# Scoring two time steps at once in four 32-column tiles, with the gated recurrence 14 slots behind

## The reference, cut to what matters

```python
hist, news = inputs[:, :-1, :], inputs[:, -1, :]
hs = _gru(hist, gru_W, gru_U, gru_b)                       # 50 sequential steps
emb = concat([hs, news - hs, news, hs * news])             # attention
a = relu(emb @ att_W1 + att_b1)                            # 512 -> 128
a = relu(a @ att_W2 + att_b2)                              # 128 -> 64
ats = sigmoid(a @ att_W3 + att_b3)                         # 64 -> 1, the score
def au_step(h, xs):                                        # gated recurrence, 50 steps
    u, r = sigmoid(xu_t + h @ au_Uu), sigmoid(xr_t + h @ au_Ur)
    c = tanh(xc_t + r * (h @ au_Uc))
    u_ = at_t * u
    return (1.0 - u_) * h + u_ * c
x = batchnorm(concat([h_final, news]))                     # then the head:
x = leaky(x @ d_W1 + d_b1); x = leaky(x @ d_W2 + d_b2); y = sigmoid(x @ f_W + f_b)
```

## Time and profile before

| | us |
|---|---|
| median of 3 runs | 1956.56 (1956.45 to 1956.91) |
| the profiled execution | 1956.07 |
| its span | 1954.2 |
| PE busy | 1930.7 (99%) |
| POOL, DVE, ACT busy | 1627.2, 1501.8, 1458.8 |

### The profile page before, as it was taken

The page is one execution under the profiler, slowest core; times in us unless marked ns, Lnnn a source line. Parts: engine busy times, 40 slices in busy tenths (PEclk is TensorE's granted clock), DMA queues, the critical chain, the costliest instruction groups (busy, mean ns, idle before and its releaser), DMA issues. The chain is left out here.

```text
span 1954.2 us, 29732 instructions
## 1 busy us (share of the span) xinstructions
PE 1930.7 (99%) x9190; PEld 859.3 (44%) x9190; DVE 1501.8 (77%) x2355; ACT 1458.8 (75%) x2466; POOL 1627.2 (83%) x1387
## 2 busy tenths in 40 slices
PE   8999999999999999999999999999999999999988
PEld 3344444444444444444444444444444444444433
DVE  7877777777777777777777777777777777777875
ACT  7877777777777777777777777777777777777764
POOL 7788888888888888888888888888888888888762
PEclk9999999999999999999999999999999999999999
DMA  3121111111111111111111121111111111111010
GB/s 127 50 71 49 49 70 52 50 49 70 48 48 70 49 51 52 70 48 48 54 65 48 49 69 53 49 49 70 48 48 70 48 52 50 70 48 48 33 44 22
DMA packets 37577, 108.12 MB, mean 55 GB/s; under 512 B 4329, under 2 KB 4585, under 8 KB 31153
## 3 DMA queue, kind: packets, MB, share of 16 engines
q1 hardware_dynamic: 37410, 107.57, 15.5%
q10 hardware_dynamic: 144, 0.26, 0.0%
HBM read 107.39 MB, written 0.42 MB: 55 GB/s over the span
## 5 line engine op out<-in xcount | busy, mean ns | idle before, releaser
L949 PE MATMUL ps<-h_hi,w_hi 128*128 128x512 f16 x1384 | 525.2, 380 | 11.4 <-DVE g L722 6.7
L951 PE MATMUL ps<-h_hi,w_lo 128*128 128x512 f16 x1384 | 524.5, 379 | 0.0
L950 PE MATMUL ps<-h_lo,w_hi 128*128 128x512 f16 x1384 | 524.5, 379 | 0.0
L304 POOL TENSOR_TENSOR hn_lo<-hn,hn_hi 128x512 f16<-128x512 f32 x200 | 232.6, 1163 | 183.4 <-ACT hn_hi L420 183.3
L298 POOL TENSOR_TENSOR hn<-h,news 128x512 f32<-128x512 f32 x200 | 255.3, 1277 | 74.6 <-DVE h L846 74.5
L569 ACT ACTIVATE ps<-gt,p_rest 128x512 f32<-128x512 f32 x196 | 135.3, 690 | 216.4 <-DVE gt L843 216.4
L370 POOL TENSOR_TENSOR gus<-gu,score 128x512 f32<-128x512 f32 x197 | 249.9, 1268 | 5.2 <-DMA score<-score_rows 3.6
L363 POOL TENSOR_TENSOR g_lo<-g,g_hi 128x512 f16<-128x512 f32 x196 | 228.0, 1163 | 18.9 <-ACT g_hi L594 17.6
L834 DVE TENSOR_TENSOR gt<-gr,ps 128x512 f32<-128x512 f32 x196 | 134.7, 687 | 140.2 <-ACT gr L597 140.2
L317 POOL TENSOR_TENSOR x_lo<-x,x_hi 128x512 f16<-128x512 f32 x196 | 227.4, 1160 | 15.1 <-ACT x_hi L440 10.6
L377 POOL TENSOR_TENSOR d<-h,hc 128x512 f32<-128x512 f32 x186 | 236.9, 1274 | 0.4 <-ACT hc L590 0.4
(11 more groups left out here) (131 smaller groups left out, 3728.2 us busy)
## 6 DMA issues: line engine op xcount, KB each, us to landing
score<-score_rows SPq DMA_DIRECT2D x50, 1024.0 KB, 4.6
x<-in_xs SPq DMA_DIRECT2D x199, 256.0 KB, 3.1
news<-in_xs SPq DMA_DIRECT2D x4, 256.0 KB, 5.1
score_rows<-s_rows SPq DMA_DIRECT2D x50, 8.0 KB
p_rest<-in_pack_rest SPq DMA_DIRECT2D x1, 776.0 KB, 6.6
p_att<-in_pack_att SPq DMA_DIRECT2D x1, 290.0 KB, 5.2
x<-in_xs ACTq DMA_DIRECT2D x1, 256.0 KB, 4.1
p_gru<-in_pack_gru SPq DMA_DIRECT2D x1, 195.0 KB, 4.3
```

The lines of the kernel that those rows point to most:

```text
L304: g.tensor_tensor(hn_lo[:, k, :], hn[:, k, :], hn_hi[:, k, :], ALU.subtract).then_inc(hnlo_ready, 1)
L949: m.matmul(ps[:, bank, :], w_hi[:, w, :], hi, start=start, stop=False)
L950: m.matmul(ps[:, bank, :], w_hi[:, w, :], lo, start=False, stop=False)
L951: return m.matmul(ps[:, bank, :], w_lo[:, w, :], hi, start=False, stop=stop)
```

## The change

- `BLOCK` = 8 items (two steps) are scored together. Layer-two activations get four buffers instead of two (`a2_hi`, `a2_lo`), `w3_pair` is 128x32, and `scores` makes 8 matmuls once in eight slots, in four column tiles of 32. `s_rows` then holds eight rows; SP stores them once per two steps and spreads them by two DMAs of four rows each, with a semaphore each; `score` has eight chunks.
- LAG 10 -> 14, HIST (ring of h parts, and loop body) 12 -> 16 slots: the loop covers slots 20 to 195 in 11 passes; EARLY = 18. So slots 4 to 13 are without gated part, 14 to 17 with 6 matmuls of it, 18 to 199 are full, 200 to 214 hold the rest.
- Start: `p_gru` comes in two DMAs (reset weights and biases first). Item 0 is done with three fp32 matmuls straight from `p_gru` and `x32`, without splits. The update gate of the first four items has four PSUM banks. WARM 10 -> 7. The second load of x chunk 0 waits for `z_pe`.
- Slots from 200 are written apart (`late`): products `gxh` of the gated part alternate between two banks (`gxh_bank`), so PE waits for the state two items back and not one; the last scores are made at slot 203 in bank B_A1.
- Batch norm: three Newton rounds of three small DVE operations; two of the small operations in each of slots 18, 19 and 196 to 199, in the middle of the slot, three more in slots 200 to 202. The scale goes into the first head weights (`w_d1`, split in fp16), the shift into the bias by four tiny matmuls; `news_bn` and the scaled states are gone.
- Head: the first layer uses split fp16 products, except two fp32 ones for the last state. ACT computes the leaky branch from PSUM, DVE the other and the maximum. `head_out` runs once for all chunks, at four 32-row offsets of one bank.

```diff
-    LAG = 10
-    HIST = 3 * NC
-    LOOP_LO = 4 * NC
+    LAG = 14
+    HIST = 4 * NC
+    BLOCK = 2 * NC
+    LOOP_LO = 5 * NC
...
-            def scores(count):
+            def scores(count, bank=B_SCORE):
                 for p in range(2):
                     pe.wait_ge(a2lo_ready[p], count)
                 for part in (a2_hi, a2_lo):
-                    for p in range(2):
-                        done = m.matmul(ps[p * H:(p + 1) * H, B_SCORE, :], w3_pair[:, :], part[:, p, :],
+                    for q in range(NC):
+                        done = m.matmul(ps[32 * q:32 * (q + 1), bank, :], w3_pair[:, :], part[:, q, :],
                                         start=part is a2_hi, stop=part is a2_lo)
-                done.then_inc(score_pe, NC)
+                done.then_inc(score_pe, BLOCK)
...
+            def spread_scores(scored, stored, first_used, second_used):
                 sp.wait_ge(s_ready, scored)
+                if first_used is not None:
+                    sp.wait_ge(gus_ready, first_used)
+                sp.dma_start(score_rows[:, :], s_rows[0:P:P // BLOCK, :]).then_inc(rows_stored, 16)
                 sp.wait_ge(rows_stored, stored)
-                sp.dma_start(score[:, :, :], score_rows.partition_broadcast(P)).then_inc(score_landed, 16)
+                sp.dma_start(score[:, 0:NC, :], score_rows[0:NC, :].partition_broadcast(P)).then_inc(score_landed[0], 16)
+                if second_used is not None:
+                    sp.wait_ge(gus_ready, second_used)
+                sp.dma_start(score[:, NC:, :], score_rows[NC:, :].partition_broadcast(P)).then_inc(score_landed[1], 16)
...
+            pe.wait_ge(gru_landed, 16)
+            pe.wait_ge(x_landed[0], 16)
+            first_item(B_R0[0], "Wr", r_pe)
+            pe.wait_ge(input_landed, 16)
+            first_item(B_XH0[0], "Wh", xh_pe)
+            first_item(B_Z0[0], "Wz", z_pe)
...
+            def late(low):
+                item = low - LAG
...
+                if low == ITEMS:
+                    pe.wait_ge(g_ready, item)
+                elif low == ITEMS + 1:
+                    pe.wait_ge(t1_ready, ITEMS)
+                else:
+                    pe.wait_ge(g_ready, item - 1)
+                split_product(gxh_bank(item), GW_C, *hg, start=True, stop=True).then_inc(gxh_pe, 1)
...
+            def head_1_state(c):
+                pe.wait_ge(glo_ready, ITEMS - NC + c + 1)
+                for k in range(2):
+                    split_product(B_D1[c][k], D_1 + k, g_hi[:, c, :], g_lo[:, c, :], start=False, stop=True).then_inc(d1_pe, 1)
+            def head_out():
+                pe.wait_ge(y2_ready, NC)
+                for c in range(NC):
+                    done = m.matmul(ps[32 * c:32 * c + 1, B_F, :], p_rest[:, PACK_REST["F"]], y2[:, c, :],
+                                    start=True, stop=True)
```

More of the change, by code:

```diff
@@ L271, in _ @@
                 load_step(3, c)
-                if c == 2:
-                    spread_scores(NC, None, 16)
-            with sp.Fori(4, T) as step:
+            for c in range(NC):
+                load_step(4, c)
+                if c == 1:
+                    spread_scores(BLOCK, 16, None, None)
+            for c in range(NC):
+                load_step(5, c)
+            xs_next = xs[1:, :, :]
+            with sp.Fori(6, T, 2) as step:
                 for c in range(NC):
@@ L621, in head_2 @@
                 act.wait_ge(d2_pe, c + 1)
[L622 to L634 removed]
+                a.activation(y2p[:, c % 2, :], ps[:, B_D2[c % 2], :], ACT.Identity,
+                             bias=b_leak[:, 2:3], scale=LEAKY).then_inc(y2p_ready, 1)
@@ L636, in _ @@
+            for s in range(ITEMS, ITEMS + LAG):
+                late(s)
+            late(ITEMS + LAG)
+            head_1(1)
+            head_2(0)
+            head_1(2)
+            head_2(1)
+            head_1(3)
+            head_2(2)
+            head_2(3)
+            head_out()
         @block.vector
@@ L811, in slot @@
                 if pairs_of(low - 1):
-                    low_2(1, paired(s0 + (off - 1)))
+                    low_2(1, low - 1, paired(s0 + (off - 1)))
                 if has(low):
@@ L943, in _ @@
+            for s in range(ITEMS, ITEMS + LAG):
+                late(s)
+            late(ITEMS + LAG)
+            for k in range(2):
+                head_1(1, k)
+            head_2(0)
+            for k in range(2):
+                head_1(2, k)
+            head_2(1)
+            for k in range(2):
+                head_1(3, k)
+            head_2(2)
+            head_2(3)
         @block.tensor
@@ L1243, in _ @@
-            for s in range(LOOP_HI, LAST):
-                slot(s - s % NC, s % NC)
-            head_1_state(0)
-            for c in range(1, NC + 3):
-                if c < NC:
-                    head_1_news(c, 0)
-                    head_1_news(c, 1)
-                    head_1_state(c)
-                if 0 <= c - 1 < NC:
-                    head_2(c - 1)
-                if 0 <= c - 2 < NC:
-                    head_out(c - 2)
+                m.matmul(ps[:, bank, :], dw2[:, 0, :], y1[c % 2][:, 0, :], start=True, stop=False)
@@ new lines, in head_2, with head_out @@
+                m.matmul(ps[:, bank, :], dw2[:, 1, :], y1[c % 2][:, 1, :], start=False, stop=True).then_inc(d2_pe, 1)
+            def head_out():
+                pe.wait_ge(y2_ready, NC)
+                for c in range(NC):
+                    done = m.matmul(ps[32 * c:32 * c + 1, B_F, :], p_rest[:, PACK_REST["F"]], y2[:, c, :],
+                                    start=True, stop=True)
+                done.then_inc(f_pe, 1)
+            for s in range(LOOP_HI, ITEMS):
+                slot(s - s % NC, s % NC)
@@ L1257 @@
+            for s in range(ITEMS, ITEMS + LAG):
+                late(s)
+            head_1_news(1, 1)
+            head_1_state(1)
+            head_2(0)
+            head_1_news(2, 0)
+            head_1_news(2, 1)
+            head_1_state(2)
+            head_1_news(3, 0)
+            head_1_news(3, 1)
+            head_2(1)
+            last_state()
+            head_2(2)
+            head_2(3)
+            head_out()
 def kernel(**inputs):
```

578 lines of the change are left out of this document (366 added, 212 removed).

## The result

| | before | after |
|---|---|---|
| median, us | 1956.56 (1956.08 to 1958.45, 5 runs) | 1948.19 (1946.67 to 1948.36, 5 runs) |
| span of the profiled execution | 1954.2 | 1946.4 |

The ratio is 0.9954, with a 95% interval of 0.994 to 0.9969: 8.4 us faster, where 19.6 were forecast. The time lies in the range, the mechanism that put it there is not the forecast's.

What follows compares the result with a forecast made beforehand. PE was taken to bound the loop, dependencies the rest; -10.8 + 2.3 + 0 + 1.1 - 1.0 - 3.5 - 0.4 - 6.8 = -19.1 us from 1956.07 gave 1937, range 1928 to 1949.

Steps and rivals of the forecast that it cites:

- What bounds the kernel: Inside the loop PE is always busy, so only the number of matmuls and changes of form count; outside, dependencies.
- part 1: Scores: four 32-column tiles run side by side, -10.8 us; one more change of form per two steps, +2.3.
- part 3: LAG 14: four added early slots bring idle time, +1.1 us; the longer loop body makes no difference.
- The rival that says so: Loop body outgrows what an engine holds, instruction fetches stall each back edge: 1945 to 1963 us, chance 0.08.
- Part 4: Start: item 0 by three fp32 products of 0.86 each, four update-gate banks: -1.0 us, bounds 0 and -2.5.
- the bound that was named 0: End of the start's range in which ACT's chain begins as before and nothing is gained.
- Part 5: Batch norm operations spread over six slots: -3.5 us, leaving 1.0 in slots 196 to 199, 0.3 in 18 and 19.
- Part 6: Gated tail from state 199: DVE's order sets 4.24 us per gated state, sum 71.4, change -0.4 us.
- Part 7: Head, last gated state to end: 16.6 us instead of 23.4, a change of -6.8.
- two exclusive cases: Head: `head_out`'s four fp32 one-column matmuls run side by side, 15.6 us to the end, or not, 18.2.
- Part 2: Score store and its two spreading DMAs: no cost, taken as 0; up to 1.2 us on POOL per two steps.

Runs made afterwards that it cites:

- experiment 7: Kernel after plus 60 one-column DVE memsets ahead of the loop, with `scores` issued twice: 1947.29 us, a pass of 153.08.
- experiments 6, 10 and 12: Kernel after plus 60 DVE memsets, with 10 warm-up matmuls (1955.01 us), 13 warm-up matmuls (1953.37), or seven and three 16-column matmuls behind them (1958.97).
- experiment 12: Kernel after plus 60 DVE memsets, seven warm-up matmuls and three 16-column PE matmuls behind them: 1958.97 us, ratio 1.0023.
- experiments 1 and 2: Kernel after with 60 or 20 one-column DVE memsets ahead of its first wait: 1937.89 us with 60, 1949.04 with 20.
- experiment 5: Kernel after with the four batch norm operations of slots 18 and 19 moved to slot 196: 1938.99 us, ratio 0.9907.
- experiments 9 (one more warm-up matmul) and 11: Kernel after plus 60 DVE memsets, with WARM 8 (1937.44 us), or WARM 10 and twenty 16-column PE matmuls behind the warm-up (1937.07).
- that of 3: Kernel after with 10 warm-up matmuls instead of 7, no memsets: 1965.44 us median, ratio 1.0057; profiled execution 1946.30.

## Why the prediction was wrong

**What bounds the kernel, and part 1:** right. The x4 groups are there, PE's timeline of one block in the kernel after:

```profile
459.31 0.38 PE L1134 MATMUL ps<-h_hi,w_lo 128*128 128x512 f16 x1
459.62 0.40 PE L1202 MATMUL ps<-a_hi,w_pair 128*32 128x512 f16 x4
459.85 0.39 PE L1202 MATMUL ps<-a_lo,w_pair 128*32 128x512 f16 x4
460.17 0.41 PE L1211 MATMUL ps<-a_hi,w_hi 128*64 128x512 f16 x2
...
461.27 0.38 PE L1211 MATMUL ps<-a_lo,w_hi 128*64 128x512 f16 x2
461.58 0.39 PE L1132 MATMUL ps<-h_hi,w_hi 128*128 128x512 f16 x1
```

0.23 between the groups, and 0.32 from 32 to 64 columns, as 0.31 into and out of the tiled form. Two steps of the undisturbed loop take 152.22 / 2 = 76.11, and 76.43 before: 0.32, close to the 0.43 - 0.095 of the forecast. The Trainium skill (TensorE: Matmul & The Clock Gate, Part 3: Packing small matmuls) has further column tiles nearly free; experiment 7 agrees, with 0.215 for a group of four.

**The failed step** is in part 3: "Loop passes show no gap, 15 or 11 make no difference." They differ by 0.93 behind each of ten back edges, 9.1 in all. The rival that says so had 0.08, with a stall of 1.7 to 3.4 and 0.7 to 2.4 uncovered; the rows show a stall of 2.9 to 3.2, 0.93 uncovered, and 1948 in its 1945 to 1963. What was argued against it, that PE has the larger body and fetched nothing, doesn't bear: DVE's body was fetched while PE's was not, and in experiments 6, 10 and 12 PE's while DVE's was not, so each engine's own body and its place decide. The body of before, 231 instructions, fits into three blocks of 128 from every place; a body of 307 does so from 384 - 307 + 1 = 78 of 128 places. The other 50, four in ten, would have been the rival's chance had the blocks been known; with two blocks of 256 it would be 50 of 256, two in ten. It was given 0.08.

The Trainium skill (Runtime: NRT & Kernel Launch, Instruction fetch mechanics) says that a taken branch out of what the engine holds stalls for a fetch. The trace agrees, with 2.88 at DVE's back edge. It gives 16 KiB blocks of 256 instructions and room for 512 instructions, 2048 on TensorE. The packets of q8 here are 16 KB, those of q14 8 KB; there the measurement decides. Room for 512 in two blocks of 256 is not refuted: it is the second reading of the table above, by which 307 instructions do not fit where they touch a third block. TensorE's 1,547 would touch eight packets of 256 in the bad places. Eight make the page's 2048 and should stay, but they were fetched again; in blocks of twice that size they would not fit. No run tells this apart either.

**Part 4, the start,** was -1.0 and came out at +2.2. The step "three fp32 products cost 0.86 each" took them at full clock, from rows late in the kernel. In the profiled execution they stand 0.85 apart, record by record, not 0.43, so each product cost 1.7. That looks like half clock: the warm-up's fp16 matmuls stand 0.43 apart, as those at a granted clock of 0.50 in experiment 12, and those from 10.49 on 0.216. (The profile's clock column says 1.00 from 0 to 14 us all the same.) With the same seven warm-up matmuls the records are 0.43 apart from the second on in experiments 1 and 2 and from the third on in 7 (state 3 at 18.28 to 18.75), and 0.85 apart almost to the end in experiment 5. What decides it from one execution to the next stays open. At full clock the part brings +0.1 and not -1.0: ACT's chain starts where it did, the bound that was named 0.

**Part 5:** -4.4 for -3.5; the operations between DVE's waits are nearly hidden: states 195 to 199 take 38.70, the same four slots of the undisturbed loop 38.33, so 0.4 are lost where 1.0 was allowed. In slots 18 and 19 PE loses 0.4 (a distance of 0.61 at 128.9 that experiment 5 doesn't have), for 0.3 forecast. **Part 6:** gated states 4.30 apart (4.24 forecast):

```profile
1899.30 0.69 DVE L836 TENSOR_TENSOR g<-g,ps 128x512 f32<-128x512 f32 x1
1903.61 0.69 DVE L836 TENSOR_TENSOR g<-g,ps 128x512 f32<-128x512 f32 x1
...
1920.44 0.70 DVE L831 TENSOR_TENSOR ps<-ps,gus 128x512 f32<-128x512 f32 x1 [0.38 <-POOL gus L375]
...
1926.44 1.40 DVE L1068 SCALAR_TENSOR_TENSOR hc<-ps,b_d,r 128x512 f32<-128x512 f32 x2
...
1931.45 0.69 DVE L836 TENSOR_TENSOR g<-g,ps 128x512 f32<-128x512 f32 x1
```

The last three are 4.66, 4.66 and 5.62 apart: twice POOL's `gus` is 0.38 late, and once two head operations stand between. The stretch took 72.4 for the 71.4 of the sum. **Part 7:** 14.26 for 16.6. PE in the head:

```profile
1935.40 1.88 PE L1406 MATMUL ps<-g,w_d 128*128 128x512 f32 x4
1939.87 1.02 PE L1417 MATMUL ps<-d,p_rest 128*128 128x512 f32 x2
1942.45 1.04 PE L1423 MATMUL ps<-news,p_rest 128*1 128x512 f32 x8 [1.56 <-DVE news L1073]
```

The eight records of `head_out` are two groups of four, 0.43 apart, and end in 1.04: side by side, the 15.6 of the working. The middle of two exclusive cases was no forecast, and it was taken wrongly too: of 15.6 and 18.2 it is 16.9, not 16.6. The rest, 1.3, is that `head_2` was through 8.6 after the last gated state and not 10.5 (PE had done more of the head before it), less 0.5 behind it. **Part 2:** right, POOL doesn't wait for the scores, line 401 has no idle time before it on the page:

```profile
540.44 0.57 SPq L276 DMA_DIRECT2D score_rows<-s_rows  x1
...
542.56 0.43 SPq L281 DMA_DIRECT2D score<-score_rows  x1
...
550.28 1.27 POOL L401 TENSOR_TENSOR gus<-gu,score 128x512 f32<-128x512 f32 x1
```

So the sum without the fetches holds: the kernel with 60 memsets has a span of 1935.5, 18.7 less than before, for 19.1 forecast, and 1937.89 us for 1937. That it fits so closely is in part luck: scores and early slots came out 1.4 worse than forecast, the start 1.1 and the tail 1.0, the batch norm 0.9 better and the head 2.3. The two kernels of experiments 9 (one more warm-up matmul) and 11, with 1937.44 and 1937.07, are as good within their ranges, and all beat the kernel after by 10 to 11 us.

Open: why PE's body, badly placed, is fetched at only some back edges (two in the profiled execution of experiment 12, three in that of 6, four in that of 10, none in that of 3), and so why such a kernel varies by 16 us and more where the others vary by 2.

## What to carry to other kernels

Where a hardware loop gets longer, or code is added ahead of it, look for instruction queues inside the loop and for "issue" waits at the first line of its body, on every engine, before anything else is explained. A loop's cost depends on its place in each engine's stream: shift it with a few idle instructions and compare, for four instructions here were worth 9 us and six took 21 away. An edit ahead of the loop, a warm-up too, is tested at more than one place, or its verdict is that of the place.

## What the runs showed of the hardware

- DVE's instructions come in 8 KB packets (q14), PE's in 16 KB (q8). A DVE body within three blocks of 128 instructions was not fetched again, one in four was, at every back edge: a stall of 2.9 to 3.2 us for DVE, and 0.93 (experiment 2: 1.12) for the pass.
- PE pays far more: 5.1 us idle (2.46 and 2.05 at "issue", and what lies around), then half clock for some 4, 7.1 us in the pass shown and 6.3 to 8.4 in all nine.
- A change between 32- and 64-column tiles costs as much as one between tiled and full, 0.1 us; four column tiles of 512 columns cost 0.215 together.
